# A graph network kernel: the codes of its node groups worked out in thirds through PSUM, low halves in pieces of four tiles, turned rows in four banks

## The reference, cut to what matters

```python
def reference(x, src, dst, W_msg, b_msg, W_ih, W_hh, b_ih, b_hh):
    # x: 12500 x 128; src, dst: 212500 edges, sorted by dst, self loops included
    def step(h, _):
        messages = h[dst] @ W_msg.T + b_msg
        agg = segment_sum(messages, src, num_segments=12500)
        gi = agg @ W_ih.T + b_ih
        gh = h @ W_hh.T + b_hh
        i_r, i_z, i_n = split(gi, 3);  h_r, h_z, h_n = split(gh, 3)
        r = sigmoid(i_r + h_r);  z = sigmoid(i_z + h_z)
        n = tanh(i_n + r * h_n)
        return (1 - z) * n + z * h, None
    h = maximum(layernorm(x), 0)
    h, _ = scan(step, h, None, length=5)
    return x + h
```

## Time and profile before

| | |
|---|---|
| median of 3 runs | 5581.22 us (5581.06 to 5582.93) |
| the profiled execution, its own time | 5582.73 us |
| its span, first to last instruction | 5580.8 us |
| PE busy | 5275.3 us (95%) |
| DVE busy | 2702.9 us (48%) |
| ACT busy | 1404.0 us (25%) |
| POOL busy | 3952.4 us (71%) |
| first scatter starts | 156.0 us |
| last scatter starts | 1018.7 us |
| first gather of the steps | 1029.4 us |

### The profile page before, as it was taken

How to read it: one execution, slowest core, us unless ns; L and a number is a source line. 1 busy time by engine, 2 the same in 40 slices (tenths; PEclk the granted TensorE clock), 3 DMA queues, 4 the chain that set the end, 5 groups by cost and what they waited for, 6 DMA issues and landing times.

```text
span 5580.8 us, 112334 instructions
## 1 busy us (share of the span) xinstructions
PE 5275.3 (95%) x40364; PEld 4034.0 (72%) x40365; DVE 2702.9 (48%) x7018; ACT 1404.0 (25%) x2081; POOL 3952.4 (71%) x4057
## 2 busy tenths in 40 slices
PE   5499997599999999999999999999999999999998
PEld 1244443487888888888878788888878888888886
DVE  8799997365555533333333333333333333333333
ACT  6799997011111111111111111111111111111110
POOL 2777777777777777677777677777767777767773
PEclk9799999799999999999999999999999999999999
DMA  5255554455655665655565566566566556565555
GB/s 161 55 143 143 143 143 117 126 169 168 179 173 171 198 181 173 182 172 171 168 198 180 175 179 175 170 186 184 175 175 177 171 175 197 174 180 174 169 171 177
DMA packets 685005, 934.75 MB, mean 167 GB/s; under 512 B 96225, under 2 KB 418525, under 8 KB 683932
## 3 DMA queue, kind: packets, MB, share of 16 engines
q1 hardware_dynamic: 489418, 675.11, 40.0%
q0 software_dynamic: 129888, 224.86, 15.1%
q10 hardware_dynamic: 65522, 32.57, 1.9%
HBM read 778.74 MB, written 153.46 MB: 167 GB/s over the span
## 4 chain that ended last, share of the span: by engine, by line
PE 73%; POOL 5%; issue 2%; DVE 2%; ACT 0%; DMA 0%; DVEq 0%; PEldq 0%; SPq 0%
PE f_ps_a L849 28%; PE f_ps_b L849 25%; POOL f_ring L605 5%; PE f_ps_a L860 4%; PE f_ps_b L860 4%; PE f_ps_m L889 2%; PE f_ps_c L871 2%; PE f_ps_deg L892 2%; PE f_ps_c L890 2%; PE f_ps_c L891 2%; PE f_ps_c L872 2%; PE f_ps_c L899 1%; PE f_ps_m L881 1%; DVE f_ring L1292 0%; POOL fast_rec L587 0%
## 5 line engine op out<-in xcount | busy, mean ns | idle before, releaser
L605 POOL DMA_INDIRECT f_ring<-fast_hrows,f_work x3365 | 3257.8, 968 | 1224.5 <-issue 1006.3
L849 PE MATMUL f_ps_a<-f_hr,f_ring 128*128 128x256 f16 x15600 | 1953.4, 273 | 82.9 <-issue 82.9
L849 PEld LDWEIGHTS f_ps_a<-f_hr,f_ring 128*128 128x128 fp8e4 x15600 | 1524.8, 98 | 294.6 <-issue 120.2
L849 PE MATMUL f_ps_b<-f_hr,f_ring 128*128 128x256 f16 x13800 | 1734.4, 273 | 0.0
L849 PEld LDWEIGHTS f_ps_b<-f_hr,f_ring 128*128 128x128 fp8e4 x13800 | 1351.6, 98 | 190.6 <-issue 34.2
L1292 DVE TENSOR_SCALAR f_ring<-f_iota_h,f_work 128x128 f16<-128x128 f16 (+1 forms) x3365 | 666.2, 285 | 1335.8 <-PE f_ps_a L860 658.6
L587 POOL DMA_INDIRECT fast_rec<-f_slots x656 | 663.9, 1012 | 235.6 <-issue 199.8
L860 PE MATMUL f_ps_a<-f_ring 128*128 128x256 f16 x2310 | 545.3, 273 | 12.1 <-DMA f_ring<-fast_hrows,f_work 12.1
L1245 DVE SCALAR_TENSOR_TENSOR f_work<-f_deg,f_bias_c,f_ps_c 128x512 f32<-128x512 f32 x125 | 93.4, 747 | 889.4 <-PE f_ps_deg L892 889.4
L1198 DVE TENSOR_SCALAR f_ring<-f_ps_m,f_work 128x256 uint16<-128x256 f16 x1536 | 505.7, 401 | 0.0
L860 PE MATMUL f_ps_b<-f_ring 128*128 128x256 f16 x2025 | 480.3, 274 | 4.1 <-DMA f_ring<-fast_hrows,f_work 4.1
(11 more groups left out here) (320 smaller groups left out, 4103.5 us busy)
## 6 DMA issues: line engine op xcount, KB each, us to landing
f_ring<-fast_adj SPq DMA_DIRECT2D x750, 640.0 KB
fast_adj<-f_ring SPq DMA_DIRECT2D x192, 512.0 KB
f_ring<-fast_hrows,f_work POOLq DMA_INDIRECT x3365
f_deg<-fast_deg SPq DMA_DIRECT2D x125, 256.0 KB
fast_hrows<-f_work ACTq DMA_DIRECT2D x124, 256.0 KB
f_hr<-fast_hrows SPq DMA_DIRECT2D x24, 640.0 KB, 6.0
fast_rec<-f_slots POOLq DMA_INDIRECT x656
fast_hrows<-f_deg SPq DMA_DIRECT2D x1, 6528.0 KB, 42.2
```

Source lines behind the costliest of these rows:

```text
L605: nc.gpsimd.indirect_dma_start(G[:, g * 2 * H:(g + 1) * 2 * H], None, hrows, bass.IndirectOffsetOnAxis(ap=idx_tab[:, col + g:col + g + 1], ...
L849: mm = pe.matmul(sums[buf][:, b * 2 * H:(b + 1) * 2 * H], lhsT=a_f8[:, t * CHUNK + b * P:t * CHUNK + (b + 1) * P], rhs=hr[:, t, :], start= ...
```

## The change

Three edits, all in the preparation.

1. *Codes.* `positions` and the instructions after it worked on all 1536 columns at a time, from SBUF to SBUF. Now they run three times over 512 columns, and the intermediate numbers lie in three PSUM banks (`ps_deg`, `ps_m`, first half of `ps_c`). Every instruction has at most one full-size input in SBUF. There are 22 instructions in each third, 66 in all, where there were 21.
2. *Pieces.* `low` runs over four tiles at a time (512 columns): 15 instructions for the first half and 10 for the second, with no wait between them. The splitting of `locT` (five linked instructions over 1536 columns) becomes 15 linked instructions over 512.
3. *Banks.* `turn_x` uses four banks in turn instead of six, since `ps_c` holds the codes' numbers meanwhile.

```diff
-                    nc.scalar.copy(hT[:, 4 * n * P:4 * n * P + w], six[n % 6][:, 0:w]).then_inc(lnT_copied, 1)
+                    nc.scalar.copy(hT[:, 4 * n * P:4 * n * P + w], six[n % 4][:, 0:w]).then_inc(lnT_copied, 1)
...
-                    if n >= 6:
-                        pe.wait_ge(lnT_copied, n - 5)
+                    if n >= 4:
+                        pe.wait_ge(lnT_copied, n - 3)
...
-                        mm = pe.transpose(six[n % 6][:, j * P:(j + 1) * P], xbuf[:, t, :], ident[:])
+                        mm = pe.transpose(six[n % 4][:, j * P:(j + 1) * P], xbuf[:, t, :], ident[:])
...
-                nc.vector.scalar_tensor_tensor(out=to[:, :, H:2 * H], in0=xbuf[:, first:last, :], scalar=SCALE, in1=to[:, :, 0:H],
-                                               op0=ALU.mult, op1=ALU.subtract).then_inc(lo_ready, 1)
+                for t in range(first, last, 4):
+                    n = min(t + 4, last)
+                    ins = nc.vector.scalar_tensor_tensor(out=to[:, t - first:n - first, H:2 * H], in0=xbuf[:, t:n, :], scalar=SCALE,
+                                                         in1=to[:, t - first:n - first, 0:H], op0=ALU.mult, op1=ALU.subtract)
+                ins.then_inc(lo_ready, 1)
...
-            g_f, g_q, g_a = (work[:, v * GK * P:(v + 1) * GK * P].bitcast(F32) for v in range(3))
+            in_node, in_whole, in_rest = ps_deg[:], ps_m[:], ps_c[:, 0:CHUNK]
+            whole_i, rest_i = in_whole.bitcast(I32), in_rest.bitcast(I32)
+            g_a = work[:, 0:GK * P].bitcast(F32)
             dve.wait_ge(groups_loaded, 16 * 2 * GK)
-            positions(sg, g_f, g_q, g_a, sg)
-            link(nc.vector.tensor_scalar(g_q.bitcast(I32), sg, CHUNK - 1, None, ALU.bitwise_and))
-            link(nc.vector.tensor_copy(g_a, g_q.bitcast(I32)))
-            dve.drain().then_inc(codes_ready, 1)
...
-            link(nc.vector.scalar_tensor_tensor(out=g_q, in0=sg, scalar=float(GJ), in1=g_f, op0=ALU.mult, op1=ALU.add))
...
+            for b in range(GK // 4):
+                part = slice(b * CHUNK, (b + 1) * CHUNK)
+                g_f, g_q = g_a[:, part], code_f[:, part]
+                beyond = sg.bitcast(U16)[:, 2 * b * CHUNK:(2 * b + 1) * CHUNK]
+
+                link(nc.vector.tensor_copy(in_node, sg[:, part]))
+                link(nc.vector.tensor_scalar(whole_i, in_node, 1.0 / T1, 0.5 / T1 - 0.5, ALU.mult, ALU.add))
+                link(nc.vector.tensor_copy(g_q, whole_i))
+                link(nc.vector.scalar_tensor_tensor(out=g_f, in0=g_q, scalar=-float(T1), in1=in_node, op0=ALU.mult, op1=ALU.add))
+                link(nc.vector.tensor_scalar(in_whole, g_f, float(T1), None, ALU.is_ge))
+                link(nc.vector.scalar_tensor_tensor(out=in_rest, in0=in_whole, scalar=-float(T1), in1=g_f, op0=ALU.mult, op1=ALU.add))
+                link(nc.vector.tensor_tensor(g_q, g_q, in_whole, ALU.add))
...
+                link(nc.vector.tensor_scalar(beyond, in_node, float(N1), None, ALU.is_ge))
+                link(nc.vector.copy_predicated(g_f, beyond, in_node))
+                link(nc.vector.tensor_copy(rest_i, g_f))
+                link(nc.vector.tensor_scalar(whole_i, rest_i, CHUNK - 1, None, ALU.bitwise_and))
+                link(nc.vector.tensor_copy(loc_f[:, part], whole_i))
+                if b == GK // 4 - 1:
+                    dve.sem_inc(codes_ready, 1)
...
+                link(nc.vector.tensor_copy(in_node, dg[:, part]))
...
+            dve.sem_inc(codes_ready, 1)
...
-            link(nc.vector.tensor_copy(pairT_i, locT))
-            link(nc.vector.tensor_scalar(byteT.bitcast(I32), pairT_i, 1, None, ALU.bitwise_and))
...
+            for b in range(GK // 4):
+                part = slice(b * CHUNK, (b + 1) * CHUNK)
+                link(nc.vector.tensor_copy(pairT_i[:, part], locT[:, part]))
+                link(nc.vector.tensor_scalar(byteT.bitcast(I32)[:, part], pairT_i[:, part], 1, None, ALU.bitwise_and))
...
```

More of the change, by code:

```diff
@@ L1159, in _ @@
-            link(nc.vector.tensor_scalar(g_q.bitcast(I32), sg, CHUNK - 1, None, ALU.bitwise_and))
-            link(nc.vector.tensor_copy(g_a, g_q.bitcast(I32)))
-            dve.drain().then_inc(codes_ready, 1)
-            link(nc.vector.tensor_scalar(sg, sg, CHUNK.bit_length() - 1, None, ALU.logical_shift_right))
-            link(nc.vector.tensor_tensor(g_f.rearrange("p (k e) -> p k e", e=P), dg.rearrange("p (k e) -> p k e", e=P),
-                                         nodeq[:, 0:GK].unsqueeze(2).to_broadcast([P, GK, P]), ALU.subtract))
@@ L1165, in _ @@
-            link(nc.vector.tensor_scalar(g_f, g_f, -1.0, float(GJ), ALU.max, ALU.min))
-            link(nc.vector.scalar_tensor_tensor(out=g_q, in0=sg, scalar=float(GJ), in1=g_f, op0=ALU.mult, op1=ALU.add))
[L1167 to L1171, removed]
@@ L1172, in _ @@
-            dve.drain().then_inc(codes_ready, 1)
+            for b in range(GK // 4):
[9 more added lines that the diff above has]
+                link(nc.vector.tensor_tensor(g_q, g_q, in_whole, ALU.add))
+                link(nc.vector.scalar_tensor_tensor(out=g_f, in0=in_rest, scalar=float(P), in1=g_q, op0=ALU.mult, op1=ALU.add))
+                link(nc.vector.tensor_scalar(beyond, in_node, float(N1), None, ALU.is_ge))
[5 more added lines that the diff above has]
+                    dve.sem_inc(codes_ready, 1)
+                link(nc.vector.tensor_scalar(whole_i, rest_i, CHUNK.bit_length() - 1, None, ALU.logical_shift_right))
+                link(nc.vector.tensor_copy(in_node, dg[:, part]))
+                link(nc.vector.tensor_tensor(in_rest.rearrange("p (k e) -> p k e", e=P), in_node.rearrange("p (k e) -> p k e", e=P),
+                                             nodeq[:, 4 * b:4 * b + 4].unsqueeze(2).to_broadcast([P, 4, P]), ALU.subtract))
+                link(nc.vector.tensor_scalar(g_f, in_rest, -1.0, float(GJ), ALU.max, ALU.min))
+                link(nc.vector.scalar_tensor_tensor(out=g_q, in0=whole_i, scalar=float(GJ), in1=g_f, op0=ALU.mult, op1=ALU.add))
+                link(nc.vector.tensor_scalar(in_rest, g_f, 0.0, NO_CODE, ALU.is_lt, ALU.mult))
+                link(nc.vector.tensor_tensor(g_q, g_q, in_rest, ALU.add))
+                link(nc.vector.tensor_scalar(in_rest, g_f, float(GJ), NO_CODE, ALU.is_ge, ALU.mult))
+                link(nc.vector.tensor_tensor(g_q, g_q, in_rest, ALU.add))
@@ L1178, in _ @@
             dve.wait_ge(codes_copied, 2 * (GK // 4))
-            link(nc.vector.tensor_copy(pairT_i, locT))
-            link(nc.vector.tensor_scalar(byteT.bitcast(I32), pairT_i, 1, None, ALU.bitwise_and))
-            link(nc.vector.tensor_scalar(byteT, byteT.bitcast(I32), float(ONE8 * 255), float(ONE8), ALU.mult, ALU.add))
-            link(nc.vector.tensor_scalar(pairT_i, pairT_i, 1, None, ALU.logical_shift_right))
-            link(nc.vector.tensor_copy(pairT, pairT_i))
+            for b in range(GK // 4):
+                part = slice(b * CHUNK, (b + 1) * CHUNK)
+                link(nc.vector.tensor_copy(pairT_i[:, part], locT[:, part]))
+                link(nc.vector.tensor_scalar(byteT.bitcast(I32)[:, part], pairT_i[:, part], 1, None, ALU.bitwise_and))
+                link(nc.vector.tensor_scalar(byteT[:, part], byteT.bitcast(I32)[:, part], float(ONE8 * 255), float(ONE8), ALU.mult, ALU.add))
+                link(nc.vector.tensor_scalar(pairT_i[:, part], pairT_i[:, part], 1, None, ALU.logical_shift_right))
+                link(nc.vector.tensor_copy(pairT[:, part], pairT_i[:, part]))
             dve.wait_ge(ln_stored, 16)
```

## The result

The changed kernel takes 5558.65 us (median of 6 runs, 5556.74 to 5560.53) against 5581.6 (6 runs, 5578.4 to 5584.32): a ratio of 0.9959, 95% interval 0.9946 to 0.9972. It is 23 us faster; 21.2 were forecast. Its profiled execution took 5558.33 us with a span of 5556.3.

The account below looks back on a forecast made before the run. POOL's scatters, held up by DVE, were taken to bound the preparation. Gains of 12.5 (codes), 8.1 (low halves) and 0.6 (splitting) make 21.2 us, from a median of 5581.22 to 5560.0 us, range 5554 to 5571.

Parts of the forecast that it names:

- What bounds: Preparation: it ends when POOL has issued its 656th scatter; DVE instructions hold POOL up, 27 us lost early.
- The codes on POOL: POOL's scatters beside the codes: 0 lost instead of 12.5 us, as instructions with a PSUM operand leave POOL at its pace.
- The codes on DVE: DVE's 66 instructions of 512 columns: 0.755 us each, 49.8 us in all against 28.3, ending at 212.4 instead of 190.9.
- The low halves: low(0) and low(1) in pieces: 9.1 and 5.8 us on DVE, POOL loses 4.2 us instead of 12.3, 8.1 won.
- Splitting locT: Five DVE instructions become 15 shorter ones, 6.9 us with links: POOL loses 1.0 us instead of 1.6, 0.6 won.
- Lateness: Path to the build: later codes, four banks and longer splitting start it some 9 us later, flag at 961, at no cost.
- the slack: Time from SP's flag store on the build path to POOL's last scatter: shrinks from 66 to about 36 us.
- The sum: Whole kernel: 12.5 + 8.1 + 0.6 = 21.2 us won, giving 5560.0 us, 0.38% faster.
- Pieces without gaps: Rival, low halves: DVE goes from piece to piece without letting POOL in; 11.6 us won, 5570 us; chance 0.09.
- PSUM holds POOL too: Rival, codes: PSUM instructions also hold POOL, 22 us lost instead of 12.5, total 5580 to 5582 us; chance 0.05.
- The build becomes the bound: Rival, SP's wait for flag and stores: decides once codes come 36 us later than forecast, the slower side; chance 0.02.
- The steps differ: Rival, steps after the preparation: they begin at another moment and change by some us either way; chance 0.04.

Follow-up runs that it names:

- codes_only: Changed kernel with the low halves and the splitting of locT put back as in the kernel before: 5568.36 us, ratio 0.9977.
- pieces_only: Kernel before, with only the low halves in pieces of four tiles and the splitting in thirds added: 5571.77 us, ratio 0.9984.
- thirds_sbuf: Changed kernel with the three PSUM arrays of the codes moved to SBUF, same 66 instructions: 5559.58 us, ratio 0.9961.
- as_changed: The changed kernel run again without edit, on the chip of the first four experiments: 5560.07 us, ratio 0.9960.
- late_build: Changed kernel plus 104 linked PSUM-to-PSUM copies of 512 columns behind the codes: 7495.67 us against 7491.3 for the kernel before, ratio 1.0001.
- four_kinds: Changed kernel plus 22 linked DVE instructions of four kinds on unused memory behind the codes, to see which hold POOL; no total given, chips at 7478 to 7515 us.
- halves_sbuf: Changed kernel with the codes in two halves of 768 columns, all in SBUF: 5.4 us lost beside the codes; no total given, chips at 7478 to 7515 us.
- quarters_sbuf: Changed kernel with the codes in four quarters of 384 columns, all in SBUF: 5.4 us lost beside the codes; no total given, chips at 7478 to 7515 us.

## Why the prediction was right, step by step

- **What bounds.** Right: POOL's last scatter, before and after. The gain of each experiment on the first chip is what its POOL lost less: 12.5 lost less and 13.4 won (codes_only), 9.7 and 10.0 (pieces_only), 20.8 and 22.2 (thirds_sbuf), 22.4 and 21.7 (as_changed).
- **The codes on POOL.** 0 lost, as taken. The forms that no row had shown, PSUM to PSUM and SBUF to PSUM, are free for POOL (late_build, four_kinds). What the prediction did not see is that most of the 12.5 would also have been won from SBUF in thirds. It said only that PSUM would do it; that PSUM was needed would have been wrong by 11 of 12.5 us, and only on this beat (halves and quarters lose 5.4).
- **The codes on DVE.** 0.69 to 0.70 us an instruction (0.73 for COPY_PREDICATED) and 0.73 with its link, not 0.755: 48.2 us instead of 49.8. The row with 0.741 was one with a bias column; the plain forms are all 0.69.
- **The low halves.** 9.12 and 5.97 us for 9.1 and 5.8; a held scatter 1.50 with a period of 1.80, as derived. Lost 3.34 instead of 4.2, since low(1) met two scatters and not three, and the edges of both stretches hold a part of a period.
- **Splitting locT.** 0.57 lost for 1.0.
- **Lateness.** The flag is 6.6 us later, not 9, and only in part for reasons that the prediction counted. DVE's last step before the build began 6.4 us later:

```profile
224.33 1.97 PE L794 MATMUL f_ps_a<-f_ident,f_work 128*128 128x128 f32 x8 [0.94 <-ACT f_hT L662]
236.25 0.43 DVE L1186 COPY f_ps_m<-f_iota_h 128x256 f32<-128x256 f32 x1 [1.36 <-DMA fast_hrows<-f_ring]
```

```profile
231.17 1.10 PE L794 MATMUL f_ps_a<-f_ident,f_work 128*128 128x128 f32 x8 [0.53 <-ACT f_hT L662]
242.69 0.43 DVE L1211 COPY f_ps_m<-f_iota_h 128x256 f32<-128x256 f32 x1
```

  (First before, then after.) The turned codes came 5.0 us later instead of 7.3: the codes ended 0.9 earlier than forecast, and PE's turning of them started 6.8 later but took 2.8 us instead of 4.9, at a granted clock of 1.00 (2.4 GHz) where it was 0.57, mostly the 1.2 GHz level, before; PE had just been turning x for 5 us, busy 4.95 of 5.4, before only 3.5 of 8. The splitting took 2.8 longer, not 2. And before, DVE had waited 1.36 us more for the stored rows, which the prediction left out; after, the splitting ends last: 5.0 + 2.8 - 1.4 = 6.4. ACT's four-bank copies of the second half took 6.1 us instead of 4.8, 1.3 for the 1 forecast. That the forecast erred on the late side cost nothing, as all of it lies in the slack. The slack is 37 us as read; that it would carry 37 us of delay was not shown.
- **The sum.** 1.3 us less lost than forecast, 1.2 from a slightly faster pace, 0.7 back from a later start of the scatters: the last scatter at 995.8 instead of 998, and 23 us instead of 21. The mechanism was right; that the median came within 1.3 us of the forecast is partly luck, since the steps of the changed kernel alone differ by 3.6 between its two traces.
- **Rivals.** "Pieces without gaps" fell (1.50, never 8). "PSUM holds POOL too" fell (969 ns). "The build becomes the bound" did not happen on this chip, and the build did end last on two others. "The steps differ": from the last scatter to the end it is 4560.5 to 4564.1 us in the six traces of chips at 5580, without order by kernel, so it moved the time by up to 3.6 us and not by the change.

## What to carry to other kernels

Where POOL issues many small DMAs and is the last to finish, lay its timeline over DVE's: scatters longer than the undisturbed one name the DVE instructions that hold it. Give those a PSUM operand (a two-source instruction for one of its inputs, a copy for its input or output), or cut them so that they fall in beat with the DMAs. The longer time on DVE, here 48 us instead of 28, costs nothing while DVE has slack. Shorter is not better by itself: work out the period, whole instructions until the DMA asks again, and choose the length that just fits.

## What the runs showed of the hardware that was not expected

- DVE instructions without any wait between them still let a waiting scatter in at every boundary. The period is then a whole number of instructions: 1.34, 1.41, 1.80, 1.47 and 1.74 us for two to six tiles each, of four, three, three, two and two pieces.
- The walk behind the forecasts of halves_sbuf and quarters_sbuf used two holding points. A scatter is held about 0.12 us after its start by both kinds of instruction, and just before its end again by one that goes from SBUF to SBUF with one source: the scatter of 162.94 took 1.75, of which 0.5 belong to the first point and 0.3 to the second. As an estimate, holding points 0.12 and 0.86 us after the start, laid over DVE's rows, give back every scatter beside the codes of before, halves_sbuf and quarters_sbuf to 0.04 us (66 of them; 12.5, 5.6 and 5.6 us lost for 12.5, 5.4 and 5.3 there), and all but two of thirds_sbuf. The two points, and how far ahead an instruction must have begun to hold, were fitted to these same rows. For the short splitting instructions of after the same numbers give 0.1 us instead of 0.6, so they are not the whole rule. The Trainium skill (SBUF — State Buffer, Who interferes with whom) has it that two inputs take only the read side of the shared ports and that descriptors need the write side, the latter as an inference. Here two inputs alone held scatters for 7.8 us; if the page is right on the inputs, a scatter needs the read side too.
- The hold works both ways: in thirds_sbuf two-source instructions of 0.69 us took 0.77 with a scatter just started, and one-source ones of 0.43 up to 0.62.
- Two chips of three ran this kernel, and every variant, in about 7490 us instead of 5580. While the scatters ran, PE was busy 127 of 760 us there; when they had ended, 608 of 630 (windows of halves_sbuf, 300 to 1060 and 1070 to 1700). That is less than half of it: in halves_sbuf the first gather starts 737 us later than in as_changed, and from there to the end it is 5758 us instead of 4553, with PE busy 86% of the steps instead of 99%. Why was not found.
